# Expert stage of an eight-stage kernel on one core: tile table in two parts, row loads ahead of the down weights, down products four tiles behind their gates

## The chip, the cores and the metric

One core of one Trainium2 chip runs the whole program once. The metric is the device time of one execution in microseconds, as a median of several runs. The engines are TensorE (PE, with PEld for its weight loads), VectorE (DVE), ScalarE (ACT), GpSimd (POOL) and SyncE (SP); SP, ACT and POOL also issue DMAs.

## The reference, cut to what matters

The model is four pairs of an attention-like block and a feed-forward block on x of shape 8 x 256 x 256 (8 items of 256 tokens). The change touches the second pair: an attention block with 16 heads, and a mixture of experts.

```python
def _L1_ffn_ref(x, gate_w, Wg, Wu, Wd, cWg, cWu, cWd):     # 32 experts of width 96, 16 of width 128, top 4
    w, sel = _routing(x, gate_w)                           # top 4 of 32 experts, weights normalized
    # for each token and each of its 4 experts e:
    #   w * ( silu(x Wg[e]) * (x Wu[e]) ) Wd[e]
    #   + 0.05 * w * ( silu(x cWg[e//2]) * (x cWu[e//2]) ) cWd[e//2]
...
x = _layernorm(x + _L1_attn_ref(x, w_qkv, w_o))
x = _layernorm(x + _L1_ffn_ref(x, ...))
```

## The kernel before, in words

Each of the eight blocks is a phase with its own instruction streams for five engines; between phases all engines meet in a barrier, after each has drained. Only the phases l1_attn and l1_ffn are touched.

**l1_attn** works on 8 items of 16 heads. Each engine walks over the same steps, one head entering per step; a head passes through seven stages in seven steps (projection, scores, softmax, split, sums, low part, output product). On PE, step s does the projection of head s, the scores of head s-1 (which wait for DVE's qk_split, L1258), the output product of head s-6 (which waits for DVE's val_low, L1279) and the sums of head s-4. DVE does about eight operations per step, and in some steps more: the residual and its statistics at step 6 (L135, L146, L150), the normalization at step 8, the routing of the item before at steps 0, 3 and from 15 on. Routing (class Routing) finds each token's four experts (select), gives each of the 2048 x 4 pairs its place within its expert by a triangular matmul (rank) and writes row numbers (number, L3825 to L3832). POOL then scatters the tokens' rows by indirect DMA (scatter, L1337), eight DMAs an item, into a buffer in DRAM sorted by expert, with a room of 2048 rows for each. Those of items 0 to 5 are issued within the phase, paced by the heads. The first four of item 6 are issued at the end of the phase (L1101, L1102), just ahead of POOL's last instruction, the rstd of item 7. SP loads the gate and up weights into the place of the attention weights as these come free.

**l1_ffn** begins with the routing of item 7. DVE counts rows per expert, works out a table of 95 tiles (which expert, which 128 rows), L1615 to L1642, and ACT stores it to DRAM and loads it back into one partition (L1572 to L1575), for SP (rowi) and PE (rowp) to read as registers. DVE next works out the mixing weights wk and the row numbers back for the next phase (L1644 to L1677, some 40 operations), and only then enters its tile loop. POOL issues four scatters of item 6, small fills, and, once item 7 has its numbers, eight more. SP starts the load of the down weights dL (3 MB) first, waits for the table and for all 64 scatters, and then loads tiles of 128 rows into six buffers.

The tile loop runs 95 tiles. In iteration t PE does the gate and up products of tile t (L1520, L1523), reads the registers of tile t+1, transposes the rows of tile t+2 (L1503), transposes the activated tile t-1 (L1534) and does the down product of tile t-2 (L1547, L1548), the first of which waits for dL. ACT does the silu, the copy of the turned rows and the copy of the finished tile; DVE does the product a (L1720, L1721) and the copy aT (L1729), and in iterations 8 to 73 one step of a rounding of weights for a later phase. SP stores finished tiles.

Of the kernel before, what the change touches and what calls it, by code (L numbers as in the profile page):

```python
# [967 lines left out]
def l1_attn(nc, sh, w):  # L968
# [8 lines left out]
    with ExitStack() as ctx:  # L977
# [14 lines left out]
        consts_cleared, consts_ready, gw_loaded = ph.semaphores("consts_cleared consts_ready gw_loaded")  # L992
# [52 lines left out]
        def _(sp):  # L1045
# [13 lines left out]
            routes.load_small_down(sp, 0, NH // 2)  # L1059
            sp.wait_ge(qk_ready, ITEMS * NH)  # L1060
# [6 lines left out]
        def _(pool):  # L1067
# [11 lines left out]
            pool.wait_ge(consts_cleared, 6)  # L1079
# [21 lines left out]
            pool.wait_ge(routing.idx_ready, ITEMS - 1)  # L1101
            scatter(nc, pool, sh, ITEMS - 2, 0)  # L1102
# [3 lines left out]
        def _(pe):  # L1106
# [5 lines left out]
            def item(i, p, steps, first=False, second=False):  # L1112
# [4 lines left out]
                for step in steps:  # L1117
# [17 lines left out]
                    if h_out is not None:  # L1135
# [107 lines left out]
        def _(dve):  # L1243
# [6 lines left out]
            def item(i, p, steps, first=False, second=False):  # L1250
                done = lambda h: i * NH + h + 1
                for step in steps:
# [65 lines left out]
                    if step == 3 and not first and not second:  # L1318
                        routing.number(dve, i - 2, p, i - 2)
                    if step == NH + 2:  # L1320
                        routing.number(dve, i - 1, 1 - p, i - 1)

# [8 lines left out]
def scatter(nc, pool, sh, i, j, pace=None, begun=0):  # L1331

    routes = sh.routes
    for k in range(routes.TOPK):
        if pace is not None:
# [3 lines left out]
            in_=sh.X[:, i, j, :], in_offset=None).then_inc(routes.rows_out, 16)  # L1339
# [17 lines left out]
def l1_ffn(nc, sh, w):  # L1357
# [10 lines left out]
    XL, YO = 6, 4  # L1368
    with ExitStack() as ctx:
# [5 lines left out]
            "silu_ready a_ready a_turned aT_kept down_ready y_kept sub_ready ex_ready back_ready dve_steps quant_steps")  # L1375
        x_in = ph.semaphores(" ".join(f"x_in{n}" for n in range(XL)))
# [12 lines left out]
        spot = ph.sb("spot", [P, TT, TOPK])  # L1389
# [10 lines left out]
        last_e = ph.sb("last_e", [P, 4, E])  # L1400
        begun = ph.sb("begun", [P, 4, E])
        start_e = ph.sb("start_e", [P, E])
        cols = ph.sb("cols", [P, 8])
# [8 lines left out]
        aT = [ph.sb(f"aT{n}", [P, 2, P]) for n in range(2)]  # L1412
# [5 lines left out]
        assert RT % RC == 0 and QC * QS <= TILES  # L1418
        wb, mag = (ph.sb(n, [P, RC, D], BF16) for n in ("wb", "mag"))
# [2517 lines left out]
```

## Time and profile before

| | us |
|---|---|
| median of 3 runs | 2541.62 (2540.76 to 2543.98) |
| the profiled execution | 2540.14 |
| its span, first to last instruction | 2538.4 |
| mean granted TensorE clock | 0.936 of full |
| l1_attn, last product of the last head | 884.20 |
| l1_ffn, first instruction of PE | 894.74 |
| l1_ffn, first gate product | 923.07 |
| l1_ffn, last down product begins | 1200.81 |

Times in the trace are microseconds from the start of the span. A row of the timeline gives start, duration, engine, line, operation, output and inputs, count, and in brackets how long the engine sat idle before it and what ended that. PE's ends are modelled; starts are the ones to compare.

### The profile page before, as it was taken

Reading aid. Unit: us, or ns where it says so; the run is one execution under the profiler, and the core shown is the slowest. Engines: PE = TensorE matmul, PEld = TensorE weight load, DVE = VectorE, ACT = ScalarE, POOL = GpSimd, SP = SyncE. Lnnn points to the kernel's source line nnn. Section 1 sums busy time; section 2 is a strip of 40 time slices with the busy share of each in tenths; the row PEclk is TensorE's granted clock in tenths of the full one; section 3 lists DMA queues with packets and bytes.
Section 4 is the critical chain, followed back from the end, with each engine's and each line's share of the span. In section 5 each row is a group of like instructions: output and inputs, shape, how many; then the busy total and the mean of one; then the engine's idle time right before and its main releaser. Section 6 shows DMA issues by size and latency. Waiting matters only on the chain. (4 is left out here: it accounts for less than half of the span.)

```text
span 2538.4 us, 47638 instructions
## 1 busy us (share of the span) xinstructions
PE 2207.6 (87%) x16423; PEld 1931.7 (76%) x16423; DVE 1672.1 (66%) x4005; ACT 1449.6 (57%) x3812; POOL 864.6 (34%) x887
## 2 busy tenths in 40 slices
PE   6887979999999849999478988899696899996997
PEld 5776868999999839998256766677685576765997
DVE  5785868888888745552488887778364555554554
ACT  5775547777777613333477676776242666563442
POOL 3321110011111220000678787768486243422000
PEclk8998989999999969999689999999798999997999
DMA  4000110000000653332411111000400000000001
GB/s 150 1 1 17 49 53 18 2 18 18 18 18 18 207 141 115 119 103 88 135 41 49 51 51 47 34 34 1 119 1 1 1 1 1 1 1 1 1 1 34
DMA packets 74223, 111.77 MB, mean 44 GB/s; under 512 B 16026, under 2 KB 59666, under 8 KB 72868
## 3 DMA queue, kind: packets, MB, share of 16 engines
q1 hardware_dynamic: 66352, 87.22, 10.7%
q0 software_dynamic: 7488, 21.50, 2.6%
q8 instruction: 136, 2.23, 0.4%
q14 instruction: 99, 0.81, 0.1%
q10 hardware_dynamic: 148, 0.01, 0.0%
HBM read 79.73 MB, written 28.97 MB: 43 GB/s over the span
## 5 line engine op out<-in xcount | busy, mean ns | idle before, releaser
L1921 POOL TENSOR_TENSOR l2a_hb<-l2a_hb,l2a_Cb 128x1024 f32<-128x1024 f32 x128 | 303.1, 2379 | 117.3 <-DVE l2a_hb L2402 116.5
L2402 DVE TENSOR_TENSOR_SCAN l2a_hb<-l2a_dA,l2a_dB 128x1024 f32<-128x1024 f32 x128 | 289.2, 2275 | 72.0 <-PE l2a_dB L2008 27.4
L2243 ACT ACTIVATE l2a_dA<-l2a_delta,l2a_An 128x255 f32<-128x255 f32 x512 | 214.5, 498 | 26.3 <-DVE l2a_delta L2331 13.8
L2008 PE MATMUL l2a_dB<-l2a_diag,l2a_dxT 64*128 64x128 f32 x2048 | 187.8, 305 | 26.1 <-DVE l2a_hb L2402 13.3
L2008 PEld LDWEIGHTS l2a_dB<-l2a_diag,l2a_dxT 64*128 64x128 f32 x2048 | 138.9, 193 | 89.3 <-PE l2a_dB L2008 37.1
L964 PE MATMUL l1a_QK<-l1a_xh,early_wqkv_h 128*128 128x256 f32 x512 | 146.6, 286 | 1.5 <-DVE l1a_xl L128 1.5
L964 PE MATMUL l1a_QK<-l1a_xh,early_wqkv 128*128 128x256 f32 x512 | 144.1, 281 | 0.0
L964 PE MATMUL l1a_QK<-l1a_xl,early_wqkv_h 128*128 128x256 f32 x512 | 143.9, 281 | 0.0
L2028 PE MATMUL l2a_YS<-ident,l2a_hb 128*128 128x128 f32 x1024 | 140.4, 283 | 1.0 <-POOL l2a_hb L1921 1.0
L1223 ACT ACTIVATE l1a_ex<-l1a_S,l1a_nm 128x256 f32<-128x256 f32 x256 | 119.3, 471 | 36.7 <-DVE l1a_nm L1275 36.7
L2028 PEld LDWEIGHTS l2a_YS<-ident,l2a_hb 128*128 128x128 f32 x1024 | 115.1, 144 | 12.1 <-POOL l2a_hb L1921 1.2
L1720 DVE TENSOR_TENSOR l1f_a<-l1f_s,l1f_GU 128x96 f32<-128x96 f32 x95 | 24.1, 254 | 140.0 <-ACT l1f_s L1590 140.0
L1258 DVE TENSOR_TENSOR l1a_qkl<-l1a_QK,l1a_qkh 128x512 fp32r<-128x512 f32 x128 | 87.9, 687 | 38.9 <-ACT l1a_qkh L1198 37.4
L3086 ACT COPY l3a_eT<-l3a_PT 128x512 f32<-128x512 f32 x96 | 56.8, 591 | 91.3 <-PE l3a_PT L2969 91.3
L3220 DVE TENSOR_REDUCE l3a_mx<-l3a_S 128x2 f32<-128x512 f32 (+1 forms) x96 | 65.6, 683 | 62.1 <-PE l3a_S L2923 62.1
L1337 POOL DMA_INDIRECT moe_x_rows<-X,routes_idx x64 | 63.7, 996 | 116.9 <-PE l1a_QK L964 86.9
L3077 ACT ACTIVATE l3a_ex<-l3a_S,l3a_nm 128x128 f32<-128x128 f32 (+1 forms) x256 | 90.6, 435 | 21.7 <-DVE l3a_nm L3223 21.6
L1523 PE MATMUL l1f_GU<-routes_over_high,l1f_xt 128*128 x380 | 99.7, 386 | 0.0
L964 PEld LDWEIGHTS l1a_QK<-l1a_xh,early_wqkv_h 128*128 128x128 f32 x512 | 97.3, 190 | 1.9 <-issue 1.9
L964 PEld LDWEIGHTS l1a_QK<-l1a_xl,early_wqkv_h 128*128 128x128 f32 x512 | 97.6, 191 | 0.0
L964 PEld LDWEIGHTS l1a_QK<-l1a_xh,early_wqkv 128*128 128x128 f32 x512 | 97.2, 190 | 0.0
L1215 ACT ACTIVATE l1a_pr<-l1a_ex,l1a_rz 128x256 f32<-128x256 f32 x128 | 65.2, 510 | 50.5 <-DVE l1a_rz L1266 47.6
(734 smaller groups left out, 7703.7 us busy)
## 6 DMA issues: line engine op xcount, KB each, us to landing
l2a_Cb<-c_rows SPq DMA_DIRECT2D x8, 2048.0 KB, 7.5
l1f_xl<-moe_x_rows SPq DMA_DIRECT2D x95, 128.0 KB, 2.0
moe_y_rows<-l1f_yo SPq DMA_DIRECT2D x95, 128.0 KB, 1.7
first_raw<-in_L_attn_w_qkv_dram SPq DMA_DIRECT2D x18, 256.0 KB, 2.8
moe_x_rows<-X SPq DMA_DIRECT2D x1, 4224.0 KB, 17.2
l1f_dL<-in_L_ffn_Wd_dram SPq DMA_DIRECT2D x1, 3072.0 KB, 16.9
X<-in_L_attn_x_dram SPq DMA_DIRECT2D x8, 256.0 KB, 6.0
routes_raw<-in_L_attn_w_o_dram SPq DMA_DIRECT2D x4, 512.0 KB, 4.2
```

The costliest lines, as they stand in the source:

```text
L964: ins = pe.matmul(out, a, b, start=(first and n == 0), stop=(last and n == len(passes) - 1), **more)
L1215: nc.scalar.activation(pr0[:, h % 2, :], ex[:, h % 2, 0, :], ACT.Copy, scale=rz[:, h % 2, 0:1]).then_inc(probs_ready, 1)
L1223: last = nc.scalar.activation(ex[:, h % 2, j, :], S[h % 2][:, j * SEQ:(j + 1) * SEQ], ACT.Exp, bias=nm[:, h % 2, j:j + 1], scale=SCALE, ac ...
L1258: nc.vector.tensor_tensor(qkl[:, h % 2].rearrange("p n t -> p (n t)"), QK[h % 2][:, :], qkh[:, h % 2].rearrange("p n t -> p (n t)").bitcas ...
L1523: last = nc.tensor.matmul(GU[t % 2][:, 2 * EI:2 * (EI + SI)], xt[t % 2][:, kc, :], wS[:, kc, :, bass.ds(small, 1), :], start=(kc == 0), st ...
L1921: nc.gpsimd.tensor_tensor(h[:, :, :], h[:, :, :], Cb[p][:, s0:s0 + UN, :], ALU.mult).then_inc(hc_ready, 1)
L2008: last = nc.tensor.matmul(out[:, m:m + 2, j * P + a:j * P + a + HP], dxT[q][a:a + HP, j, c * P:(c + 1) * P], diag[q][a:a + HP, j, s0 + m:s ...
L2028: last = nc.tensor.matmul(YS[j][:, c * P:(c + 1) * P], hb[u % RING][:, n, j * P:(j + 1) * P], sh.ident[:, :], is_transpose=True, start=Fal ...
L2243: last = nc.scalar.activation(dA[(i * NU + u) % DAS][:, n, 1:SEQ], delta[q][:, c, 1:SEQ], ACT.Exp, scale=An[:, c, s0 + n:s0 + n + 1])
L2402: nc.vector.tensor_tensor_scan(flat(hb[u % RING]), flat(dA[(i * NU + u) % DAS]), dB[u % 2][:, :], 0.0, ALU.mult, ALU.add).then_inc(scanned, 1)
L3077: last = nc.scalar.activation(ex[:, b % NB, cols], S[b % 3][:, cols], ACT.Exp, bias=nm[:, b % NB, n:n + 1])
L3220: nc.vector.tensor_reduce(mx[:, b % NB, 0:nh], S[b % 3][:, :].rearrange("p (h k) -> p h k", h=nh), AX_X, ALU.max).then_inc(max_ready, 1)
```

## The change

- The scatters of item 6 all move into l1_ffn: none is issued at the end of l1_attn. In l1_ffn POOL issues its fills first (two of them were last), then eight scatters of item 6, then eight of item 7. These 16 count on a semaphore of their own (late_rows_out).
- In l1_attn, with item 7, PE counts the rows per expert of items 0 to 5 with two small matmuls at step 1, and DVE works out a table of the first HEAD = 17 tiles in 15 steps over steps 3 to 12 (head_step, 19 operations). 17 tiles are full for certain from items 0 to 5 alone. SP stores and reloads this table in the middle of its weight loads. PE's first output product of that item waits for the first of those steps. POOL gets three more fills at the start of the phase.
- In l1_ffn SP no longer begins with dL: it needs only the head table and the scatters of items 0 to 5, loads the rows of six tiles, and then issues dL. The store of the second table stands at SP's iteration 11, its loads at 14, and the wait for it and for the late scatters at 17.
- PE transposes the rows of tiles 0 and 1 ahead of its part of the routing of item 7. The down product is four tiles behind the gate product instead of two (LAG), with four buffers aT instead of two; a store follows its row load by eight iterations instead of six (BACK).
- DVE enters the tile loop after the short start of the table. The rest of the table is done two steps per tile in tiles 0 to 3 (tabulate), the mixing weights and row numbers two steps per tile in tiles 4 to 18 (weigh). ACT's Exp for them stands in tile 4. The 66 rounding steps run in tiles 20 to 91.

```diff
@@ l1_attn
+            sp.wait_ge(head_ready, 1)
+            sp.dma_start(routes.head_dram, routes.head_i[:, :]).then_inc(head_stored, 16)
+            sp.wait_ge(head_stored, 16)
+            for dst in (routes.head_row, routes.head_expert):
+                sp.dma_start(dst[:, :], ...).then_inc(routes.head_loaded, 16)
             sp.wait_ge(qk_ready, ITEMS * NH)
...
-            pool.wait_ge(routing.idx_ready, ITEMS - 1)
-            scatter(nc, pool, sh, ITEMS - 2, 0)
             rstd(ph, pool, ITEMS - 1)
...
+                            if i == ITEMS - 1:
+                                pe.wait_ge(head_steps, 1)
...
+                    if step == 1 and i == ITEMS - 1:
+                        counts = YB[p][:, 2 * NT * routes.E:(2 * NT + 1) * routes.E]
+                        nc.tensor.matmul(counts, routes.ones[:, :], routes.run[:, 1, :], start=True, stop=False)
+                        nc.tensor.matmul(counts, routes.ones[:, :], routes.sel[:, 1, :], start=False, stop=True).then_inc(head_counted, 1)
...
+                    if 3 <= step < 3 + HEAD_OVER and i == ITEMS - 1:
+                        for n in range((step - 3) * HEAD_STEPS // HEAD_OVER, (step - 2) * HEAD_STEPS // HEAD_OVER):
+                            head_step(n, p)
...
+            def head_step(n, p):
+                if n == 0:
+                    dve.wait_ge(head_counted, 1)
+                else:
+                    dve.wait_ge(head_steps, n)
+                if n == 0:
+                    ins = nc.vector.tensor_copy(count, YB[p][:, 2 * NT * E:(2 * NT + 1) * E])
+                elif n == 1:
+                    ins = nc.vector.tensor_tensor(over, count[...], routes.full[...], ALU.is_gt)
+                elif n == 2:
+                    ins = nc.vector.tensor_reduce(tiles, over, AX_X, ALU.add)
...
@@ l1_ffn
-    XL, YO = 6, 4
+    XL, YO, AR, LAG = 6, 4, 4, 4
+    BACK = XL + LAG - 2
...
+        TAB_AT, TAB_IN = 11, 14
+        WEIGH_AT, EXP_AT, QUANT_AT = 4, 5, 20
...
+        QUANT_OVER = TILES - 3 - QUANT_AT
...
-            sp.dma_start(dL[:, :, :], w["L1_ffn_Wd"]).then_inc(down_loaded, 16)
-            sp.wait_ge(tab_loaded, 32)
-            sp.wait_ge(routes.rows_out, 16 * TT * TOPK)
-            for t in range(TILES + XL):
+            sp.wait_ge(routes.head_loaded, 32)
+            sp.wait_ge(routes.rows_out, 16 * (ITEMS - 2) * NT * TOPK)
+            for t in range(TILES + BACK):
+                if t == XL:
+                    sp.dma_start(dL[:, :, :], w["L1_ffn_Wd"]).then_inc(down_loaded, 16)
+                if t == TAB_AT:
+                    sp.wait_ge(tab_ready, 1)
+                    sp.dma_start(tab_dram, tabi[:, :]).then_inc(tab_stored, 16)
+                if t == TAB_IN:
+                    sp.wait_ge(tab_stored, 16)
...
+                if t == HEAD:
+                    sp.wait_ge(tab_loaded, 32)
+                    sp.wait_ge(routes.late_rows_out, 16 * 2 * NT * TOPK)
...
@@ pool
-            scatter(nc, pool, sh, ITEMS - 2, 1)
+            for n in range(2):
+                nc.gpsimd.memset(a[n][:, :, :], 0.0).then_inc(fill_ready, 1)
...
+            for j in range(NT):
+                scatter(nc, pool, sh, ITEMS - 2, j)
             pool.wait_ge(routing.idx_ready, 1)
             for j in range(NT):
                 scatter(nc, pool, sh, ITEMS - 1, j)
...
@@ tensor
+            routing.turn(pe, 0, 0, sh.X[:, ITEMS - 1])
+            routing.logits(pe, 0, 0)
             turn_tile(0)
             turn_tile(1)
+            pe.wait_ge(routes.head_loaded, 32)
             choose(0)
+            routing.rank(pe, 0, 0)
...
-            for t in range(TILES + 2):
+            for t in range(TILES + LAG):
...
-                if t >= 2:
-                    down(t - 2)
+                if t >= LAG:
+                    down(t - LAG)
@@ scalar
+                if t == EXP_AT:
+                    act.wait_ge(sub_ready, 1)
+                    nc.scalar.activation(ex[:, :, :], ex[:, :, :], ACT.Exp).then_inc(ex_ready, 1)
@@ vector
-                if 8 <= t < 8 + QC * QS:
-                    quantize(dve, (t - 8) // QS, (t - 8) % QS)
+                if t < WEIGH_AT:
+                    tabulate(2 * t)
+                    tabulate(2 * t + 1)
+                elif t < WEIGH_AT + WEIGH // 2:
+                    weigh((t - WEIGH_AT) * 2)
+                    weigh((t - WEIGH_AT) * 2 + 1)
+                if t >= QUANT_AT:
+                    for n in range((t - QUANT_AT) * QC * QS // QUANT_OVER, (t - QUANT_AT + 1) * QC * QS // QUANT_OVER):
+                        if n < QC * QS:
+                            quantize(dve, n // QS, n % QS)
```

## Rows read from the trace of the kernel before

**Rows 1.** Busy time by stretch: us, busy per engine, clock, DMA share, GB/s
```profile
1000.00:1100.00 100.00, 100.00 (x570) 90.74 (x569) 54.69 (x143) 37.33 (x143) 2.75 (x5) 1.00 0.36 113
```
**Rows 2.** Timeline of PE, from the phase's start to the steady loop
```profile
894.74 1.08 PE L3768 MATMUL l1f_AT<-ident,X 128*128 128x128 f32 x4 [10.27 <-PEq L3903]
...
900.89 0.21 PE L1496 MATMUL l1f_YP<-l1f_total_e,routes_ones 128*128 128x32 bf16 x1
920.23 0.66 PE L1503 MATMUL l1f_T<-ident,l1f_xl 128*128 128x128 f32 x2 [19.13 <-DMA l1f_xl<-moe_x_rows]
...
923.07 1.64 PE L1520 MATMUL l1f_GU<-routes_over_low,l1f_xt 128*128 x4 [1.04 <-ACT l1f_xt L1580]
...
935.22 0.69 PE L1534 MATMUL l1f_AT<-ident,l1f_a 128*128 128x128 f32 x2 [5.66 <-DVE l1f_a L1721]
...
940.12 0.81 PE L1520 MATMUL l1f_GU<-routes_over_low,l1f_xt 128*128 x4
...
942.94 0.81 PE L1520 MATMUL l1f_GU<-routes_over_low,l1f_xt 128*128 x4
```
**Rows 3.** The drains that end l1_attn: count, ns min/median/max, first and last start
```profile
L977 POOLq DRAIN  x1: 7102/7102/7102, 886.6 to 886.6; - x1
L977 DVEq DRAIN  x1: 769/769/769, 887.4 to 887.4; - x1
```
**Rows 4.** Timeline of POOL in l1_ffn
```profile
903.90 0.96 POOL L1337 DMA_INDIRECT moe_x_rows<-X,routes_idx  x1 [0.30 <-issue]
```
**Rows 5.** Timeline of DVE in l1_attn, item 7, steps 5 to 7
```profile
829.99 0.69 DVE L1258 TENSOR_TENSOR l1a_qkl<-l1a_QK,l1a_qkh 128x512 fp32r<-128x512 f32 x1 [0.20 <-ACT l1a_qkh L1198]
...
833.75 0.69 DVE L1258 TENSOR_TENSOR l1a_qkl<-l1a_QK,l1a_qkh 128x512 fp32r<-128x512 f32 x1 [0.43 <-ACT l1a_qkh L1198]
...
835.21 0.42 DVE L1279 TENSOR_TENSOR l1a_vl<-l1a_val,l1a_vh 128x256 fp32r<-128x256 f32 x1
...
838.66 0.66 DVE L1258 TENSOR_TENSOR l1a_qkl<-l1a_QK,l1a_qkh 128x512 fp32r<-128x512 f32 x1
```
**Rows 6.** Timeline of PE, the output product of that step
```profile
837.40 0.28 PE L964 MATMUL l1a_Y<-l1a_wo_h,l1a_vh 128*128 128x256 f32 x1
```
**Rows 7.** Timeline of DVE in l1_ffn: one table step, one product a in steady state
```profile
902.04 0.69 DVE L1616 TENSOR_TENSOR l1f_over<-l1f_n_e,l1f_thr 128x512 f32<-128x512 f32 x1
...
1190.25 0.25 DVE L1720 TENSOR_TENSOR l1f_a<-l1f_s,l1f_GU 128x96 f32<-128x96 f32 x1 [2.03 <-ACT l1f_s L1590]
```
**Rows 8.** Timeline of SP: two row loads that wait for nothing
```profile
918.15 0.38 SPq L1447 DMA_DIRECT2D l1f_xl<-moe_x_rows  x1
919.31 0.35 SPq L1447 DMA_DIRECT2D l1f_xl<-moe_x_rows  x1
```
**Rows 9.** DMA issues from 860 to 930: KB each, median us to landing
```profile
l1f_dL<-in_L_ffn_Wd_dram SPq DMA_DIRECT2D x1, 3072.0 KB, 16.9
...
l1f_xl<-moe_x_rows SPq DMA_DIRECT2D x7, 128.0 KB, 2.0
...
moe_tiles<-l1f_tabi ACTq DMA_DIRECT2D x1, 2.0 KB, 8.6
```
**Rows 10.** Busy time by short stretches at the loop's start, columns as in Rows 1
```profile
929.00:931.00 2.00, 0.56 (x4) 0.25 (x2) 1.90 (x4) 0.68 (x3) 0.00 (x0) 1.00 0.00 0
935.00:937.00 2.00, 1.78 (x7) 1.78 (x8) 0.95 (x4) 0.00 (x0) 1.64 (x2) 0.50 0.24 23
...
939.00:941.00 2.00, 2.00 (x14) 1.86 (x13) 0.79 (x3) 0.99 (x4) 0.00 (x0) 1.00 0.74 246
```
**Rows 11.** Busy time while only loads and scatters run, columns as in Rows 1
```profile
888.00:890.00 2.00, 0.00 (x0) 0.00 (x0) 0.13 (x1) 0.00 (x0) 0.00 (x0) 0.50 1.12 357
```
**Rows 12.** Timeline of ACT, a change of its function table
```profile
922.46 1.28 ACT L1589 ACT_TABLE_LOAD   x1
```
**Rows 13.** Timeline of PE, the last tile
```profile
1196.32 0.81 PE L1520 MATMUL l1f_GU<-routes_over_low,l1f_xt 128*128 x4
...
1200.81 0.60 PE L1548 MATMUL l1f_YP<-routes_over_high,l1f_aT 128*128 x2
```

More of the change, by code:

```diff
@@ L1319, in item @@
                         routing.number(dve, i - 2, p, i - 2)
+                    if 3 <= step < 3 + HEAD_OVER and i == ITEMS - 1:
+                        for n in range((step - 3) * HEAD_STEPS // HEAD_OVER, (step - 2) * HEAD_STEPS // HEAD_OVER):
+                            head_step(n, p)
                     if step == NH + 2:
                         routing.number(dve, i - 1, 1 - p, i - 1)
+            E, SE = routes.E, w["L1_ffn_cWg"].shape[1]
+            count, tiles, begins, ends, past, since = (routes.part[:, n, :] for n in range(6))
@@ L1333, in scatter @@
     routes = sh.routes
+    landed = routes.rows_out if i < ITEMS - 2 else routes.late_rows_out
     for k in range(routes.TOPK):
@@ L1467, in _ @@
                 scatter(nc, pool, sh, ITEMS - 1, j)
-            for n in range(2):
-                nc.gpsimd.memset(a[n][:, :, :], 0.0).then_inc(fill_ready, 1)
             def load_raw(c):
@@ L1491, in _ @@
         def _(pe):
-            routing.turn(pe, 0, 0, sh.X[:, ITEMS - 1])
-            routing.logits(pe, 0, 0)
-            routing.rank(pe, 0, 0)
-            pe.wait_ge(total_ready, 1)
-            nc.tensor.matmul(YP[0][:, 0:E], routes.ones[:, :], total_e[:, :], start=True, stop=True).then_inc(count_ready, 1)
             def turn_tile(t):
@@ L1583, in _ @@
             keep_tile(1)
-            for t in range(TILES + 2):
+            for t in range(TILES + LAG):
                 if t < TILES:
@@ L1660, in _ @@
-            wide = lambda n: last_e[:, n:n + 1, :].to_broadcast([P, TT, E])
-            first, room, shift, rank = (last_e[:, n, :] for n in range(4))
-            steps.did(nc.vector.tensor_scalar(first, start_e[:, :], float(P), 1.0, ALU.mult, ALU.add))
-            steps.did(nc.vector.tensor_scalar(room, nt_e[:, :], -1.0, float(P), ALU.add, ALU.mult))
-            step(nc.vector.tensor_scalar(rank, n_e[:, :], -float(P), 0.0, ALU.add, ALU.max))
-            step(nc.vector.tensor_tensor(shift, room, rank, ALU.subtract))
@@ L3725, in __init__ @@
         self.gate_up_loaded, self.small_down_loaded, self.rows_out = sh.gate_up_loaded, sh.small_down_loaded, sh.rows_out
+        self.late_rows_out, self.head_loaded = sh.late_rows_out, sh.head_loaded
+        pairs = (ITEMS - 2) * SEQ * self.TOPK
+        self.HEAD = -(-(pairs - experts * (P - 1)) // P)
+        self.head_row, self.head_expert = (sb(f"head_{n}", [1, self.HEAD * 4], I32) for n in ("row", "expert"))
+        self.head_start, self.head_tiles = (sb(f"head_{n}", [P, experts]) for n in ("start", "tiles"))
+        self.full = sb("full", [P, tiles])
+        self.ones_e = sb("ones_e", [P, experts])
+        self.tau = sb("tau", [P, 1])
+        self.head_cols = sb("head_cols", [P, 8])
+        self.head_i = sb("head_i", [P, 4], I32)
+        self.head_dram = nc.dram_tensor("moe_head_tiles", (P, 4), I32).ap()
     def load(self, sp, free):
```

263 lines of the change are left out of this document (181 added, 82 removed).

## The prediction

> **What bounds the kernel now.** I read the busy time by stretches first, to find stretches in which PE idles, then PE's timeline across them, then the engines named in its brackets. In the steady tile loop PE is busy all the time at full clock [rows 1], and one tile follows the other at 942.94 - 940.12 = 2.82 us [rows 2]. Nothing on DVE, ACT or SP can shorten that; the 66 rounding steps lie in it already and the pitch doesn't show them. So the change can only gain ahead of the steady loop, and the reader should look at what PE waits for there. Four waits stand in a row.
>
> 1. The border of the phases. PE's first instruction comes 10.27 us after its last [rows 2]. POOL's drain holds the barrier: it takes 7.10 us from 886.6 to 893.7, while DVE's, the next latest, ends at 887.4 + 0.77 = 888.2 [rows 3]. From the last drain to PE's start it is 894.74 - 893.7 = 1.0 us.
> 2. The table. From the count's matmul at 900.89 to the first turned row at 920.23 PE does nothing [rows 2]; the store of the table alone took 8.6 us to land, and dL, which was running, 16.9 us [rows 9].
> 3. DVE's block of some 40 operations ahead of its loop: PE stands 5.66 us for the first product a [rows 2].
> 4. The clock. PE's granted clock is at its lower level (0.50, 1.2 GHz) from before the phase on, up for a moment at 929, down again after the wait for DVE, and up for good only from 939 [rows 10].
>
> I count from S, PE's first instruction of l1_ffn: 894.7 before. Steady state is reached with tile 3 at 940.12; tile 5's gate product is then at 940.12 + 2 x 2.82 = 945.8, which is S + 51.1. All later tiles hang on it by the fixed pitch, so this one number is what I forecast.
>
> **The border: -5.5, and +1.6 for what the attention pays.** POOL has no scatter of item 6 in flight when it drains, since they are all issued later, so DVE's drain is next and S moves by 893.7 - 888.2 = 5.5 us [rows 3]. The price is in the 19 small operations on DVE (steps 3 to 12 of item 7). Two are 128x512 operations of 0.69 us as the like one [rows 7]; the other 17 I take at 0.2 to 0.25 each with their waits, by the neighbours of that row, together about 4.5 us. Is DVE covered? Heads 5 and 6 begin 833.75 - 829.99 = 3.76 us apart on DVE, PE's pace, and DVE idles 0.43 of them [rows 5], so it recovers about 0.4 us per step; but after the residual the next head begins 838.66 - 833.75 = 4.91 us later [rows 5], that is 1.15 us behind that pace. Carrying the new work step by step through the same recursion (1.4 us at step 4, then 0.2 to 0.5 at each) DVE would be 1.4 us late at head 5, 2.8 at head 7, 3.3 at head 9, 3.2 at head 12. PE tolerates 837.40 - (835.21 + 0.42) = 1.8 us [rows 5, 6]: its output product takes the low part that DVE finished that long before. With 0.1 for the semaphore, PE slips by 3.3 - 1.7 = 1.6 us. The bounds are 0 (each 0.2 us operation falls into a gap) and 3. The two counting matmuls and PE's added wait cost nothing: their data are there a step earlier. SP's added waits, with a store and two loads of 2.0 us each [rows 9], stand ahead of weight loads that wait for PE's step 15 anyway; if they came late, the first gate product has room until S + 6.
>
> **From S to the down weights.** SP issues row loads 919.31 - 918.15 = 1.1 us apart [rows 8]; the first at S + 1.0, the sixth at S + 6.5, dL at S + 6.9. The first two rows land 2.0 us after their issue [rows 9], by S + 4.1, and PE turns them within the time in which DVE selects. The count's matmul stands at 900.89 - 894.74 = S + 6.2 [rows 2] as before; the first gate product follows at S + 6.4. Without a down product a tile costs PE 2.82 less 0.87 (two of them lie 0.44 apart), 1.95 us at full clock, twice that at the lower level. Before, the clock rose 5.8 us after the gate products began (923.07 to about 929) [rows 2, 10]. From the first gate product to the end of the fifth there are 9.1 us of work at full clock: 5.8 us do 2.9 of it, 6.2 remain, so PE is through at S + 18.4. DVE is in its loop by then: its start of the table ends near S + 10.6, the first product a is wanted by PE at S + 13.
>
> In iteration 4 PE wants tile 6's rows and then dL itself. Both are late. The row load of tile 6 is issued behind dL on SP's queue. dL took 16.9 us with 12 scatters beside it [rows 9]; now there are 16, without a pause, one in 0.96 + 0.30 = 1.26 us [rows 4], from about S + 1.8, behind the fills, to S + 22. I take 19 us; the lower end is 3.1 MB at the 357 GB/s of loads and scatters together [rows 11], 9 us, the upper 22. That gives S + 25.9 and, with 0.8 us for the row behind it, PE resumes at S + 26.7 after 8 us of idling. A turn, a turn and a down product are 1.3 us, then tile 5's gate product. The clock falls in the wait, as it did in that of 5.66 us; there PE resumed at 935.2 and got the upper level at 939 [rows 2, 10], 4 us at half speed, so a loss of 2.0; I take 2.5. Tile 5 stands at S + 26.7 + 1.3 + 2.5 = S + 30.5, against S + 51.1: -20.6.
>
> The Trainium skill (DMA: Bandwidth & Descriptors, Queues, rings and completion order) says that an engine takes the descriptors of one queue in ring order and alternates between queues. By it tile 6's rows must wait for dL; no row of before shows a load behind a long one on SP's queue. If it did not hold, dL itself would still hold the down product a few matmuls later, and the sum would be the same within 0.3 us.
>
> **What is hidden.** Late scatters: the last landed about 4 us after its issue, so S + 26, and SP asks for them at its iteration 17, over ten tiles later. The second table is stored at 11 and asked for at 16 or 17. Exp in ACT's tile 4 needs two changes of the function table, 1.28 us each [rows 12], behind DVE's two operations of 0.69; counted from the resumption, silu of tile 5 is done at + 5.1, its product a at + 5.6, and PE wants it at + 5.9. It just fits; where it doesn't, it is 1 or 2 us once. Of the tiles with DVE's larger work the worst (tile 7) has four 0.69 us operations on top of 0.95: 3.8 us against 2.82. DVE idles 2.03 us per tile [rows 7], and the tiles behind are lighter. The rounding has at most one step a tile, as before. Stores and loads on SP keep their distance from the down product. The steady pitch doesn't change: LAG moves a down product and adds none.
>
> **The tail: +1.2.** Two more down products follow the last gate product. Before, the last gate product at 1196.32 had 4.5 us to the last down matmul at 1200.81 [rows 13]; two more add 2 x 0.87 = 1.7, and about 0.5 us of waits for a and aT that stood in it go.
>
> **Sum**, for the profiled execution of 2540.1: -5.5 + 1.6 - 20.6 + 1.2 = -23.3, 2516.8. The runs' median lies 1.5 us above the profiled one, so 2518.3 in the metric; I say 2518.
>
> **The rivals.**
> A. The down weights are there in time. If dL lands within 11 us of its issue (9 us by the bound above), PE never stops: tile 5 at S + 18.4 + 1.3 = S + 19.7, no second fall of the clock, -31.4 in place of -20.6: 2507.5. Against it: the same load took 16.9 with fewer scatters beside it. For it: a good part of those 16.9 could be the scatters' bursts. 13%.
> B. The start is worse than that: DVE's two-step tiles and ACT's Exp delay the products a after the resumption, each wait costs PE its clock again (3.4 us lost for 7 at half speed), or the attention slips by 3. Together 5 to 15 us: 2523 to 2533. 17%.
> C. The loop itself gets slower. PE's sequencer now keeps the register pairs of five tiles instead of three, and the down product waits for aT, the free bank and the store at another place. If this shows as more than 23.3 / 91 = 0.26 us per tile, the gain is gone; at 0.35 it is 91 x 0.35 = 32 us and 2550. For it: SP and PE are paced by each other's semaphores. Against it: PE's rows stand without a gap, so 0.26 us needs a new wait in every tile, and no distance shrinks. 4%, and 4% that it comes out near nothing.
> D. The change doesn't do what it says at the border: POOL's drain is long for another reason than the four scatters, and S stays: 5.5 less, 2524. Inside B's share.
>
> **Chances.** Forecast (2512 to 2523) 62%, A 13%, B with D 17%, no change 4%, slower 4%. A change under 0.2%, 5 us, can't be told from none here. So faster 0.92, same 0.04, slower 0.04. The range: half of A below and the far part of B with C above may be left out: 2508 to 2526.
>
> **What would show it.** Right: POOL's drain under 1 us; PE's first instruction of l1_ffn near 890.8; first gate product 6.4 us behind it; five gate products, then one wait of PE of 5 to 10 us on tile 6's row; dL landing 17 to 21 us after its issue; tile 5 near 921; pitch 2.82 to the end. Wrong: no such wait (A); waits on DVE's a or ACT's copies in tiles 5 to 12 (B); a pitch over 2.9 (C); heads 5 to 12 of item 7 at their old pace would lower the attention's price to 0.

## The result, and the profile after

The changed kernel takes 2522.3 us (median of 4 runs, 2521.5 to 2524.64) beside 2541.19 for the kernel before on the same chip: ratio 0.9925, 95% interval 0.9912 to 0.9938. That is 18.9 us less; the prediction said 2518, that is 23.3 less. The profiled execution has a span of 2520.0 us (2538.4 before) and 2521.75 us in the metric.

Single executions differ by up to 5 us in stages that no kernel here changes (PE enters the attention at 368.4 to 373.8 us). So I compare stages by their own length, each between two first instructions of PE: A, the attention with the border behind it, from PE's first attention instruction to S; and F, the expert stage, from S to PE's first instruction of the SSM stage.

| | A | F | tile 6's gate product |
|---|---|---|---|
| before | 524.23 | 329.67 | S + 53.8 |
| after | 524.54 | 312.67 | S + 35.3 |
| forecast of the change | -3.9 | -19.4 | S + 33.3 |
| measured change | +0.3 | -17.0 | |

The forecast named tile 5; with the clock up again tile 6 stands one pitch of 2.82 behind it, and I use tile 6 because tile 5 may still run at the lower clock. So the stage gave nearly what was expected, and the attention with its border nothing. PE's timeline of the changed kernel (start, duration, line, operation, out<-in, idle before and what ended it) answers to [rows 2]:

```profile
369.12 1.11 PE L106 MATMUL l1a_T<-ident,l1a_xin 128*128 128x128 f32 x4 [6.62 <-POOL l1a_xin L96]
...
885.45 0.28 PE L964 MATMUL l1a_Y<-l1a_wo_h,l1a_vl 128*128 128x256 f32 x1
893.66 1.09 PE L3923 MATMUL l1f_AT<-ident,X 128*128 128x128 f32 x4 [7.93 <-PEq L4060]
...
900.01 1.64 PE L1609 MATMUL l1f_GU<-routes_over_low,l1f_xt 128*128 x4
...
909.45 0.91 PE L1609 MATMUL l1f_GU<-routes_over_low,l1f_xt 128*128 x4 [1.47 <-ACT l1f_xt L1670]
...
918.43 0.69 PE L1623 MATMUL l1f_AT<-ident,l1f_a 128*128 128x128 f32 x2 [6.00 <-DVE l1f_a L1857]
...
928.98 0.81 PE L1609 MATMUL l1f_GU<-routes_over_low,l1f_xt 128*128 x4
...
931.80 0.81 PE L1609 MATMUL l1f_GU<-routes_over_low,l1f_xt 128*128 x4
...
1176.73 0.81 PE L1609 MATMUL l1f_GU<-routes_over_low,l1f_xt 128*128 x4
...
1182.78 0.60 PE L1637 MATMUL l1f_YP<-routes_over_high,l1f_aT 128*128 x2
1206.33 1.11 PE L106 MATMUL l2a_Y<-ident,l2a_xin 128*128 128x128 f32 x4 [22.95 <-POOL l2a_xin L96]
```

The 19 us wait in [rows 2] is gone, and the first gate product stands 6.35 us behind S. The prediction calls that wait the table's. In the kernel before two things ended it close together, as SP's waits between 893 and 925 us show (line, what for, us in total, times, longest):

```profile
SPq L1441 <- DMA moe_x_rows<-X,routes_idx: 21.1, 1, 21.1
SPq L1446 <- DMA l1f_rowp<-moe_tiles: 1.0, 1, 1.0
```

SP had waited 21.1 us for the last scatter and waited 1.0 us more for the table. So an earlier table alone would have gained some 1 us there (an estimate from these two rows). The wait could go only because SP no longer waits for the late scatters either.

PE's gap at the border is 7.93 us in place of 10.27. From tile 6 on the pitch is (1176.73 - 928.98) / 88 = 2.815 us, as before. But the wait between 909 and 918 isn't for a row or for dL, as the prediction had it: it is for DVE's product a. ACT, DVE and SP in the same stretch, from their timelines:

```profile
906.09 0.25 ACT L1679 ACTIVATE l1f_s<-l1f_GU 128x96 f32<-128x96 f32 x1 [5.84 <-PE l1f_GU L1612]
...
908.93 0.37 ACT L1670 COPY l1f_xt<-l1f_T 128x256 f32<-128x256 f32 x1 [2.42 <-DMA first_raw<-in_L_attn_w_qkv_dram]
917.47 0.25 ACT L1679 ACTIVATE l1f_s<-l1f_GU 128x96 f32<-128x96 f32 x1 [8.17 <-DMA l0f_raw<-in_L_attn_w_qkv_dram]
...
908.93 0.19 DVE L1729 TENSOR_REDUCE l1f_cols<-l1f_begun 128x1 f32<-128x32 f32 x1 [1.76 <-remote]
...
917.92 0.26 DVE L1856 TENSOR_TENSOR l1f_a<-l1f_s,l1f_GU 128x96 f32<-128x96 f32 x1 [8.61 <-ACT l1f_s L1680]
...
894.68 9.93 SPq L1539 DMA_DIRECT2D l1f_xl<-moe_x_rows  x6
904.63 0.00 SPq L1523 DMA_DIRECT2D l1f_dL<-in_L_ffn_Wd_dram  x1
908.19 9.17 SPq L1539 DMA_DIRECT2D l1f_xl<-moe_x_rows  x3
```

ACT starts its second silu at 917.47, although the gate product that it needs was done by 905.2; the loads named as its releasers ended hundreds of microseconds earlier, so what released it isn't in the trace. DVE's 8.61 us follow from ACT's, since its product takes that silu. But before that ACT and DVE resume together at 908.93, SP's first six row loads are stretched over 10 us, and its next three, behind dL, over 9. I call this standing: engines stop together, for nothing that the trace names, while POOL issues scatters.

The drains that end the attention (count, ns min/median/max, first and last start) answer to [rows 3]:

```profile
L977 POOLq DRAIN  x1: 4768/4768/4768, 887.8 to 887.8; - x1
L977 DVEq DRAIN  x1: 769/769/769, 888.7 to 888.7; - x1
```

POOL's last scatter was issued at 870, 17 us earlier, and the drain still takes 4.77 us. It is still the last, 3.2 us behind DVE's.

### The profile page after: what moved, and what is told of

The parts are those of the page before. It is cut to its first block and busy times, and to the rows that moved or that the text cites. A ratio compares the mean times of both kernels' runs of the same rounds, so it can differ in the third digit from the quotient of the medians.

```text
span 2520.0 us, 47681 instructions
## 1 busy us (share of the span) xinstructions
PE 2211.0 (88%) x16425; PEld 1934.0 (77%) x16425; DVE 1676.7 (67%) x4036; ACT 1452.5 (58%) x3814; POOL 865.1 (34%) x890
## 3 DMA queue, kind: packets, MB, share of 16 engines
q1 hardware_dynamic: 66648, 87.23, 10.8%
## 5 line engine op out<-in xcount | busy, mean ns | idle before, releaser
L2152 PE MATMUL l2a_dB<-l2a_diag,l2a_dxT 64*128 64x128 f32 x2048 | 187.8, 305 | 26.2 <-DVE l2a_hb L2546 13.3
```

The source lines that it names most:

```text
L2152: last = nc.tensor.matmul(out[:, m:m + 2, j * P + a:j * P + a + HP], dxT[q][a:a + HP, j, c * P:(c + 1) * P], diag[q][a:a + HP, j, s0 + m:s ...
```

## Experiments: is the stage what the prediction said?

**The changed kernel once more.** No edit.

> The changed kernel itself once more. In its first profiled execution ACT stood 8.17 us ahead of 917.47 and DVE 8.61 ahead of 917.92 within dL's transfer, and SP issued its first six row loads in 9.9 us; in two variants that leave this part of the code alone (small down weights later, down products two tiles behind) ACT did not stand and SP took 6.7 us. Theory Once: the standing belongs to that one execution; now ACT starts its second silu within 12 us of PE's first instruction S of the stage, PE works through five gate products by S + 18 and then waits some 8 us for tile 6's row or dL, as the prediction had it, with tile 5's gate product at S + 27 to S + 31. Theory Placed: it belongs to this very program; ACT stands 6 to 9 us again and tile 5 is at S + 32.5. Time 2519 to 2525 either way.

Measured: 2522.71 us, 0.9918 (0.9894 to 0.9941). A 524.47, F 310.17. The engines don't stand this time. PE's and SP's timelines:

```profile
897.86 1.09 PE L3923 MATMUL l1f_AT<-ident,X 128*128 128x128 f32 x4 [7.92 <-PEq L4060]
...
904.22 1.64 PE L1609 MATMUL l1f_GU<-routes_over_low,l1f_xt 128*128 x4
907.78 0.82 PE L1609 MATMUL l1f_GU<-routes_over_low,l1f_xt 128*128 x4
...
913.64 0.82 PE L1609 MATMUL l1f_GU<-routes_over_low,l1f_xt 128*128 x4
...
924.71 0.69 PE L1591 MATMUL l1f_T<-ident,l1f_xl 128*128 128x128 f32 x2 [9.39 <-DMA l1f_xl<-moe_x_rows]
...
930.61 0.81 PE L1609 MATMUL l1f_GU<-routes_over_low,l1f_xt 128*128 x4
...
898.88 6.61 SPq L1539 DMA_DIRECT2D l1f_xl<-moe_x_rows  x6
905.54 0.45 SPq L1523 DMA_DIRECT2D l1f_dL<-in_L_ffn_Wd_dram  x1
```

Five gate products, then one wait of 9.39 us for tile 6's row behind dL: theory Once. The first profiled execution lost 2.5 us of F to the standing, which does not come in every execution of this program. What makes the engines stand stays open; two more executions below show it.

**The down product two tiles behind.**

```
-    XL, YO, AR, LAG = 6, 4, 4, 4
+    XL, YO, AR, LAG = 6, 4, 2, 2
```

> Same work; the down product follows its gate product by two tiles as in the kernel before, not four; all else is as in the changed kernel. By the prediction (PE works through five gate products and then waits for dL) the first down product is wanted two tiles earlier, PE does two gate products fewer beside the load, and steady state comes 4 us later, less 1.2 us at the end: 2524 to 2526. Theory Packets: PE is held by ACT until 918 either way, and dL is in at 920, so the down products wait for nothing: steady state as before or up to 1 us later, and the end 1.2 to 1.7 us earlier: 2520.5 to 2522.5.

Measured: 2524.15 us, 0.9934 (0.9918 to 0.9951); A 524.55, F 313.48, 3.3 more than in the repetition. PE now stops two tiles earlier, and for dL itself:

```profile
918.41 1.22 PE L1636 MATMUL l1f_YP<-l1f_dL,l1f_aT 96*128 x2 [11.16 <-DMA l1f_dL<-in_L_ffn_Wd_dram]
```

Tile 6 is 4.3 us later and the end 1.0 us closer to it, near the forecast's "4 us later, less 1.2 us at the end". Theory Packets falls, the prediction's account holds. The intervals of the two ratios overlap; it is the stage's length that tells them apart.

**dL ahead of the rows.**

```
+            sp.dma_start(dL[:, :, :], w["L1_ffn_Wd"]).then_inc(down_loaded, 16)
             sp.wait_ge(routes.head_loaded, 32)
 ...
-                if t == XL:
-                    sp.dma_start(dL[:, :, :], w["L1_ffn_Wd"]).then_inc(down_loaded, 16)
```

> Same work; dL is issued first in the expert stage, as in the kernel before, and the six row loads stand behind it; all else is as in the changed kernel. By the prediction's reasoning the rows then land behind dL's packets, 15 us after its issue, so the first gate product is near S + 17 in place of S + 6.4 and tile 5 later by 1 to 4 us, since the five tiles are no longer worked off beside the load: 2523 to 2527. Theory Packets adds: ACT, DVE and SP stand 2 to 8 us each within S + 2 to S + 17, where little is due, and run freely afterwards, so that the change's gain from rows ahead of dL is small: at most 3 us, 2522 to 2525. If the order of rows and dL were what carries the gain (9 us or more), the time would be 2531 or more.

Measured: 2528.25 us, 0.9946 (0.9923 to 0.9969); A 524.51, F 314.81, 4.6 more than in the repetition. PE's first row is late:

```profile
913.74 0.69 PE L1590 MATMUL l1f_T<-ident,l1f_xl 128*128 128x128 f32 x2 [14.60 <-DMA l1f_xl<-moe_x_rows]
```

Here S is 895.47, so the first row is turned at S + 18.3. A row load behind dL on SP's queue waits for it, which no row of the kernel before showed. The order is worth 4.6 us, the later down product 3.3. If the parts add up, which no run shows, some 12 of the stage's 19.5 us are left for the table in two parts, the late scatters that SP no longer waits for, and DVE's work spread over the tiles; these weren't taken apart.

**The last small weights later.**

```
             routes.load(sp, ((0, 3 * part),))
-            routes.load_small_down(sp, NH // 2, NH)
 ...
                 if t == XL:
+                    routes.load_small_down(sp, SE // 2, SE)
                     sp.dma_start(dL[:, :, :], w["L1_ffn_Wd"]).then_inc(down_loaded, 16)
```

> Same work; the last load of the attention's SP block, the second half of the small experts' down weights (512-byte packets, 888 to 892.2 us), is issued in the expert stage instead, just ahead of dL. Theory Drain waits for transfers: POOL's drain, 4.77 us from 887.85 to 892.6, lasts until the outstanding loads are in. Then it ends near 889.5, PE's first instruction of the expert stage moves from 893.66 to about 890.5, and the time falls by 3 us to 2519, if the stage's start keeps its distances. Theory Own length: the drain is 4.8 us long for a reason on POOL. Then it ends at 892.6 as before and PE starts at 893.7; time 2521.5 to 2525, since dL comes a little later.

Measured: 2524.38 us, 0.9931 (0.9914 to 0.9947); A 524.56, F 313.65. The drain doesn't move, the wait grows:

```profile
L977 POOLq DRAIN  x1: 4767/4767/4767, 889.7 to 889.7; - x1
```
```profile
925.74 0.69 PE L1591 MATMUL l1f_T<-ident,l1f_xl 128*128 128x128 f32 x2 [12.66 <-DMA l1f_xl<-moe_x_rows]
```

These loads under way aren't what the drain waits for: theory Own length. And what is put ahead of dL is paid for: dL lands 20.8 us after its issue in place of 17.9, and F is 3.5 us longer.

## Experiments: what sets the length of dL

**dL in short packets.**

```
-                    sp.dma_start(dL[:, :, :], w["L1_ffn_Wd"]).then_inc(down_loaded, 16)
+                    for e in range(0, E, 4):
+                        sp.dma_start(dL[:, e:e + 4, :], w["L1_ffn_Wd"][:, e:e + 4, :]).then_inc(down_loaded, 16)
 ...
-                    pe.wait_ge(down_loaded, 16)
+                    pe.wait_ge(down_loaded, 16 * (E // 4))
```

> Same work; the down weights dL come as 8 loads of 4 experts each (4 KB per partition) in place of one load with 32 KB per partition, at the same place of SP's order. Theory Packets: in the changed kernel dL's long packets fill the DMA engines from 905 to 920 us, and ACT (idle 8.17 us before 917.47), DVE (8.61 before 917.92) and SP (next row load 3.56, 4.26 and 4.90 us behind the last) stand because something of theirs that comes by DMA waits behind those packets. Then with short packets ACT's and DVE's waits in 905 to 918 fall below 2 us each, dL lands within 10 us, and PE's next wait is for dL itself at the first down product, which starts near 916 to 920 in place of 925.29: 4 to 7 us off, 2515.5 to 2518.5 us. Theory Own cause: the engines stand for a reason of their own at the start of the loop, whatever dL does. Then ACT still starts its second silu near 917 and the time stays at 2521 to 2523.5. A third outcome, SP takes 1 us for each of 8 issues and tile 6's row comes 7 us later: 2522 to 2526.

Measured: 2522.16 us, 0.9919 (0.9903 to 0.9936); A 524.54, F 309.54. Nothing stands, but nothing stood in the repetition either, so this run says nothing on the cause. PE waits 7.86 us for tile 6's row, 1.5 less than with long packets; F is 0.6 us shorter, which is hardly clear of noise (the run with the early drain below leaves the expert stage alone and has an F 0.4 us shorter).

**The late scatters behind dL.**

```
+            pool.wait_ge(down_loaded, 16)
             for j in range(NT):
                 scatter(nc, pool, sh, ITEMS - 2, j)
```

> Same work; POOL starts the 16 late scatters only when dL is in. Theory Shared: dL takes 15 us (96 packets of 32 KB, 2.5 us each on 16 DMA engines, 206 GB/s) because scatters of 2.1 MB run beside it, all together 260 to 330 GB/s. Then dL lands 9 to 11 us after its issue at S + 7.7, near S + 18, PE hardly waits, tile 5's gate product is at S + 20 to S + 23 in place of S + 32.5, and the stage is 8 to 11 us shorter: 2511 to 2515 us. Theory Packet: a packet of 32 KB takes 2.5 us whoever runs beside it; dL stays at 15 us, tile 5 at S + 27 to S + 31, the time at 2519 to 2522. Theory Late rows: the scatters, now issued from S + 18 to S + 38, hold the row loads behind them and cost up to 5 us: 2524 to 2527.

Measured: 2522.76 us, 0.9923 (0.99 to 0.9945); A 524.48, F 309.43. From the DMA issues between 880 and 930 us (KB, us from issue to landing), the repetition first, then this kernel:

```profile
l1f_dL<-in_L_ffn_Wd_dram SPq DMA_DIRECT2D x1, 3072.0 KB, 17.9
```
```profile
l1f_dL<-in_L_ffn_Wd_dram SPq DMA_DIRECT2D x1, 3072.0 KB, 18.3
```

Without a scatter beside it dL takes as long: theory Packet (its 15 us count dL's packets alone, from the first to the last). The prediction's 19 us were right in size and wrong in their reason: it added time for scatters that cost dL nothing.

**POOL's early drain, alone, then with both edits on dL.**

```
+            nc.gpsimd.drain()
             rstd(ph, pool, ITEMS - 1)
```

> Same work; POOL gets one more drain in the attention, behind its last scatter and ahead of the last small operations, where it idles some 16 us. In the profiles POOL's drain at the end of a phase takes 0.79 us where the phase issued no software DMA, 4.77 behind 48 scatters, 5.55 behind 64 gathers, and in the expert stage 2.00 behind 24 (before) and 2.33 behind 28 (after): 0.083 us for each. Theory Count: the drain pays for each of POOL's own DMAs since the last drain; the early one takes the 4 us out of the way, the last one is 0.8 us, DVE's drain becomes the last, and the attention phase is 525.67 - 3.2 = 522.4 us long: 2519 us. Theory Phase: the long drain belongs to the end of a phase with software DMA whatever came between; 525.67 and 2522 stay.

Measured: 2518.32 us, 0.9898 (0.9873 to 0.9922); A 521.25, F 309.80. The added drain, then the ones that end the phase, then PE's start:

```profile
L1114 POOLq DRAIN  x1: 8009/8009/8009, 874.7 to 874.7; - x1
```
```profile
L977 POOLq DRAIN  x1: 819/819/819, 892.5 to 892.5; - x1
L977 DVEq DRAIN  x1: 769/769/769, 893.3 to 893.3; - x1
```
```profile
895.07 1.09 PE L3924 MATMUL l1f_AT<-ident,X 128*128 128x128 f32 x4 [4.72 <-PEq L4061]
```

The early drain takes 8 us in POOL's idle time, the last one 0.82, so that DVE's drain is the last to end, and PE's gap at the border falls from 7.9 to 4.7 us. A is 3.2 us shorter, the whole of what the prediction had expected of the border beyond the 2.3 that came.

```
+        self.spare = sb("spare", [P, 251])
         self.full = sb("full", [P, tiles])
```

and the edits of the three runs before (early drain, dL in 8 loads, scatters behind dL):

> The changed kernel with four edits that touch different terms, each to be read off in the profile by itself: an unused tile in Routes that makes the attention's tiles start 2048 bytes higher than in the kernel before (1044 in the changed one); POOL's early drain; dL in 8 loads of 4 KB per partition; and the 16 late scatters behind dL. The attention: theory Places says that an offset of 2048 bytes is as good as none, so PE's part is 515.4 us in place of 517.4, and with the drain's 3.2 the phase is 520.4 in place of 525.6; if any offset costs, 522.4. The expert stage: with scatters beside it, dL in 4 KB packets took 14 us in e1; alone, with packets of 32 KB, 16.3 in e5. Theory Long packets: packets of 32 KB run at 13 GB/s per DMA engine whatever runs beside them, while 4 KB ones were slowed in e1 by the scatters (all together 290 to 390 GB/s). Then dL takes 8 to 10 us, is in at S + 17, PE waits at most 1 us, tile 5 is at S + 20 to S + 21 (29.07 in the repetition), and the stage is 281 to 283 us in place of 290.6. Theory Slow destination: 96 partitions take dL at about 210 GB/s in any form; then dL takes 14 to 16 us, tile 5 is at S + 27, the stage 289. In all: 2508 to 2511 us by the first, 2515 to 2517 by the second.

Measured: 2515.97 us, 0.9883 (0.9861 to 0.9906), faster than both kernels; A 521.48, F 306.33. PE's wait, and the DMA engines meanwhile (busy time by stretch, columns as in [rows 1]):

```profile
915.42 0.69 PE L1594 MATMUL l1f_T<-ident,l1f_xl 128*128 128x128 f32 x2 [5.58 <-DMA l1f_xl<-moe_x_rows]
```
```profile
902.00:904.00 2.00, 2.00 (x14) 1.85 (x13) 1.89 (x12) 0.77 (x4) 0.00 (x0) 1.00 1.06 285
904.00:906.00 2.00, 2.00 (x15) 1.85 (x14) 1.27 (x9) 0.73 (x4) 0.00 (x0) 1.00 1.04 268
...
910.00:912.00 2.00, 0.00 (x0) 0.00 (x0) 0.45 (x2) 0.30 (x2) 0.00 (x0) 1.00 1.07 272
```

dL and a few rows are all that runs, the 16 DMA engines are busy throughout, and from 902 to 912 they move 264 to 285 GB/s; the wait is 5.6 us in place of 9.4. Short packets with the scatters out of the way give 3.8 us of F here, and 2.1 in the kernel of the section on the SSM stage below, whose expert stage is the same (F 308.12, PE's wait 5.99). Each alone gave 0.6 and 0.7. Theory Long packets wanted 281 to 283, Slow destination 289; in the measure of that text (drain to drain) the two executions have 286.8 and 288.6, so they lie between, nearer to the second. The spare tile did nothing (A 521.48 beside 521.25).

**dL from ACT's queue.** Early drain and scatters behind dL as above, no spare tile, and ACT issues dL in place of SP, in 8 loads (below) or, in the second kernel, in one ahead of its first copy:

```
+            load_down(0, 8)
             routing.keep(act, 0, 0)
+            load_down(8, E)
```

> The changed kernel with POOL's early drain, the late scatters behind dL, and dL issued by ACT in 8 loads of 4 KB per partition: two ahead of its first copy of the stage, six behind it; SP's queue holds the rows alone. What is to be told apart: in r1, e5 and v1 PE's one wait is for tile 6's row (9.4, 8.0 and 5.6 us), whose load stands behind dL on SP's queue; the prediction said that the order of a queue does it. Theory Queue: with dL on ACT's own queue the rows pass it, dL (14 to 15 us long, and 1 MB of rows beside it) is in at S + 16 to S + 19, PE waits for no row and at most 2 us for dL, tile 5 is at S + 20 to S + 22 (25.18 in v1) and the stage is 281 to 284 us (286.8 in v1): 2509 to 2513 us. Theory One ring: both engines' loads end in the same order of service, the rows come behind the slices, the first gate products are 2 to 6 us late, and the stage is 288 to 292 us: 2517 to 2521.

> As the run before, but dL is one load again, with 32 KB per partition, issued by ACT as the first thing of the stage. If a DMA engine serves two queues packet by packet, a row load (128 packets of 1 KB, 8 for each of 16 engines) alternates with packets of 2.5 us and takes some 15 to 20 us, as long as dL itself: the first gate product is at S + 15 to S + 21 in place of S + 6.4, and the stage is 290 to 296 us. If queues share an engine by bytes or run side by side, the rows land within 4 us, dL is in at S + 15, and the stage is 280 to 283 us.

Measured: 2532.56 us, 0.9943 (0.9928 to 0.9959), with F 319.50; and one time of 2532.43 with F 325.43. PE's first row in the former and in the latter, then the packets of ACT's queue (q10) and of SP's (q1) in the latter from 900 to 908 us (packets, MB, share of 16 engines):

```profile
901.02 0.69 PE L1591 MATMUL l1f_T<-ident,l1f_xl 128*128 128x128 f32 x2 [4.29 <-DMA l1f_xl<-moe_x_rows]
```
```profile
910.66 0.69 PE L1591 MATMUL l1f_T<-ident,l1f_xl 128*128 128x128 f32 x2 [13.91 <-DMA l1f_xl<-moe_x_rows]
```
```profile
q10 hardware_dynamic: 48, 1.57, 90.0%
q1 hardware_dynamic: 48, 0.05, 3.4%
```

The first gate product is at S + 13.3 and S + 19.6 in place of 6.4. Neither theory of the first text holds: with short packets the rows don't wait for all of dL, and they don't pass it. The second text names what does fit both: a DMA engine takes packets of the two queues in turn, so that a row's 1 KB packets pay for one of 4 or 32 KB each; in the rows above 48 packets of 1 KB run beside 48 of 32 KB. The Trainium skill (DMA: Bandwidth & Descriptors, Queues, rings and completion order) says that an engine alternates between queue rows packet by packet; the two runs agree. But the page takes a packet to hold some 9 to 17 descriptors, and here the row's records of 1 KB take their turns singly, which is what the trace shows for this chip. So nothing long may be under way on another queue while an early load is wanted.

What these runs don't show is that a second queue is worse than the first. In both, dL is issued ahead of the rows, in the changed kernel behind them. Against the run with dL first on SP's own queue, whose first gate product is at S + 21.3, the second queue is 8.0 and 1.8 us earlier. dL on ACT's queue behind the rows wasn't run.

In both the engines stand again, this time behind dL's end, with the scatters alone. PE and ACT of the run with short packets:

```profile
926.91 0.69 PE L1623 MATMUL l1f_AT<-ident,l1f_a 128*128 128x128 f32 x2 [7.33 <-issue]
```
```profile
925.95 0.25 ACT L1685 ACTIVATE l1f_s<-l1f_GU 128x96 f32<-128x96 f32 x1 [8.89 <-DMA l0f_raw<-in_L_attn_w_qkv_dram]
```

So dL's packets aren't what makes them stand. The standing happened in three of the twelve profiled executions with this loop, each time while POOL issued scatters and in the loop's first five tiles; in the others the same overlap passed without it. The cause stays open. It cost 2.5 us in the changed kernel; in these two runs PE's waits of 7.3 and 7.8 us in it are a good part of what F lost.

## Experiments: the attention's price, and drains elsewhere

**The kernel before with nine unused tiles.**

```
+        self.spare = [sb(f"spare{n}", [P, wide]) for n, wide in enumerate((68, 68, experts, experts, tiles, experts, 1, 8, 4))]
```

> The kernel before, with nine unused tiles of the sizes that the change adds to Routes (68, 68, 32, 32, 16, 32, 1, 8 and 4 numbers of 4 bytes), so that the attention's tiles lie at the addresses they have in the changed kernel; no instruction differs. In the attention PE's part lasts 514.86 us before and 517.49 after; of these 2.6 us, 2.0 come at 0.02 us per head from the tenth head on, ahead of all that the change adds, and 0.6 in the last item. Theory Places: the addresses do it; PE's part is 516.7 to 517.0 here. Theory Instructions: it is something in the program; 514.86 stays.

Measured, one time: 2546.77 us. PE's first and last attention instruction:

```profile
370.59 1.11 PE L106 MATMUL l1a_T<-ident,l1a_xin 128*128 128x128 f32 x4 [6.61 <-POOL l1a_xin L96]
```
```profile
886.39 0.28 PE L964 MATMUL l1a_Y<-l1a_wo_h,l1a_vl 128*128 128x256 f32 x1
```

That is 515.8 us. Before it is 884.20 - 370.51 = 513.7, in the changed kernel 885.45 - 369.12 = 516.3. So 2.1 of the 2.6 us come from where the tiles lie, with no instruction changed; they come as some 0.017 us per head through all eight items. This kernel was profiled once, but the same drift stands in the changed kernel ahead of the change's own steps: at the first output product of the last item PE is 1.94 us behind the kernel before here, 1.91 in the changed kernel and 1.89 in its repetition. The other 0.5 come at one head of the last item, where the change's own steps are. Theory Places. A spare tile that moves the tiles on to 2048 bytes didn't bring them back, so which property of the address counts is open.

A has one more source of differences. In the two runs with dL on ACT's queue it is 520.3 and 520.2, 1 us shorter than with the early drain alone, and nothing in the attention differs; there the granted clock is full from 6.0 us behind PE's first instruction, in the repetition from 9.0 (read in stretches of 1 us).

**Drains in the SSM stage.** On top of the fastest kernel above:

```
+                    if u == 11 and i + 1 < ITEMS:
+                        nc.gpsimd.drain()
```

> The kernel of the run before with one edit in the next phase, the SSM stage: POOL drains in each item but the last at its step 11, where no gather of its own is under way. That phase is 600.7 to 601.4 us long and ends with POOL's drain of 5.55 us, behind 64 gathers, 4.1 us behind the next latest drain (ACT's). Theory Count: the last drain falls to 0.3 to 0.8, seven drains of 1.5 us (first 3.5) fit into POOL's idle time there (6 to 7 of 37 us), and the phase is 4 us shorter, 596.7. Theory Path: POOL's product is what the scan waits for, so that some of the drains show: the phase is 597 to 606 us.

Measured: 2521.26 us, 0.991 (0.9893 to 0.9928), beside 2515.97 on the same chip without these drains. The SSM stage from PE's first instruction to the next stage's is 592.9 us in place of 582.1. In the other executions here, none of which has these drains, it took 576.1 to 586.9, so not all of the 10.8 us need be the drains'; the medians are 5.3 apart, and the expert stages of the two profiled executions 1.8. Its drains (count, ns min/median/max), those added and the last:

```profile
L2086 POOLq DRAIN  x7: 2646/6282/6801, 1297.2 to 1709.7; - x7
```
```profile
L1902 POOLq DRAIN  x1: 298/298/298, 1787.4 to 1787.4; - x1
```

The last drain does fall, from 5.54 us to 0.30. But a drain takes 6.3 us behind as few as 8 gathers and 2.6 behind none, so 0.083 us per DMA, which had fitted the drains that end the phases, is no price that can be moved about. The drains cost more than the 4 us they take off the border: theory Path. That it is POOL's product that the scan waits for is argued, not shown.

## Why the prediction was right or wrong

- **The border, -5.5.** Wrong, the largest miss. PE's gap fell by 2.3 us, 10.27 to 7.93. The failed step is "POOL has no scatter of item 6 in flight when it drains, since they are all issued later, so DVE's drain is next and S moves by 893.7 - 888.2 = 5.5 us". 4.77 of the 7.10 us had nothing to do with scatters in flight: with the last one issued 17 us earlier, and with or without the small weights' loads beside it, the drain has this length, and an earlier drain takes it away, down to 0.82. What POOL does in it stays open. Rival D was the right one for more than half of the term.
- **The attention, +1.6.** Measured +2.6, and for another reason: 2.1 by moved tiles, which the prediction had no term for, and about 0.5 by DVE's added steps. The recursion over the heads overstated these by a factor of three, although its 19 operations, by its own prices, add up to 4.8 to 5.6 us and not to 4.5. Border and attention together: +0.3 in A, where -3.9 was forecast. These 4.2 us are nearly the whole difference between the 23.3 us forecast and the 18.9 of the medians.
- **S to the first gate product, 6.4.** Measured 6.35.
- **Five gate products by S + 18.4.** In the repetition the fifth starts at S + 15.8 and PE is through at S + 17.5. Right, and 0.9 early because the clock rose sooner: 3.6 us behind the first gate product (the second, at 907.78, takes 0.82 us), where 5.8 was forecast.
- **dL in at S + 25.9, PE going on at S + 26.7.** dL was issued at S + 7.7 in place of 6.9 and took 17.9 in place of 19; PE went on at S + 26.85, after 9.4 us for which 8 were forecast. Right in size, and in part by luck: that the scatters lengthen dL was wrong, it takes 18.3 without them.
- **Tile 6 at S + 33.3.** S + 32.75 in the repetition. In the first profiled execution S + 35.3, by the standing of ACT, DVE and SP.
- **The tail, +1.2.** 1182.78 - 1176.73 = 6.05 us from the last gate product to the last down product, 4.49 in [rows 13]: +1.56. Two more products at 0.87 would be 1.74, so of the 0.5 us of waits that should have gone about 0.2 went. With LAG back at 2 the tail is 4.49 again, so it is the two products.
- **The pitch** is 2.815 us. Rival C didn't happen.
- **The sum.** F fell by 19.5 us in the repetition, where -20.6 + 1.2 = -19.4 was forecast, and by 17.0 in the execution with the standing. With A's +0.3 that is 17 to 19 us, and the medians say 18.9.
- **Rival A**, dL within 11 us of its issue, took 357 GB/s [rows 11] for what dL could have. In short packets and with almost nothing beside it the DMA engines moved 264 to 285 GB/s at full occupancy. At that rate dL's 3.1 MB alone are 11 to 12 us (an estimate), and the eight loads took 15.7 from the first one's issue to the last one's landing. So even then its condition wasn't met.

## What to carry to other kernels

When a drain holds a barrier, first look at the drains of phases that used none of the suspected resource and of those that used it long before; an early drain in the engine's idle time is a cheap test, and here a gain of 3.2 us. Issue a load that is needed early ahead of a long one: with dL ahead of the rows the first gate product came 15 us later on the same queue, and 7 and 13 us later with dL on a second queue. And compare stages by their own length, over more than one execution: tiles added to the memory map shifted a stage by 2 us with no instruction changed, and the same expert stage took 306.3 and 308.1 us in two executions.

## What the hardware showed unexpectedly

- POOL's drain at the end of the attention takes 4.77 us although its last DMA was issued 17 us earlier, and 0.82 behind an earlier drain; in phases without DMAs of POOL's own it takes 0.8.
- The same matmuls of the attention run some 0.017 us per head slower when their tiles lie 1044 bytes higher, and as much slower at 2048.
- ACT, DVE, PE and SP can stand together, ACT for 8 to 9.5 us, with no releaser in the trace while POOL issues scatters; the changed kernel showed it in one of its two profiled executions.
- Packets of two queues run one for one: 48 of 1 KB beside 48 of 32 KB in 8 us. A row load of 128 KB, 2 us alone, then had PE wait until S + 17.6.
